# A selective-scan layer with a feed-forward layer on one core: the work behind the scan for the final 128 positions in two halves

## The reference

```python
xn = x * rsqrt(mean(x * x) + 1e-6) * norm_w
xn = xn * sigmoid((xn @ select_proj_w.T + select_proj_b) * select_gate)
xp = xn @ x_proj_w.T                       # delta | B | C, 128 columns each
delta = softplus(xp[..., :R] @ dt_proj_w.T + dt_proj_b)
A = -exp(A_log)                            # 512 x 128
def step(h, inp):                          # h: 2 x 512 x 128, one step per position
    dt, bt, ct, xt = inp
    h = exp(dt[:, :, None] * A) * h + (dt * xt)[:, :, None] * bt[:, None, :]
    return h, einsum('bdn,bn->bd', h, ct)
x1 = layernorm(x + (y + x * D_param) @ out_proj_w.T)
out = layernorm(x1 + (silu(x1 @ w_gate.T) * (x1 @ w_up.T)) @ w_down.T)   # hidden size 2048
```

## Time and profile before

| what | value |
|---|---|
| median of three runs | 2907.8 us (2907.03 to 2912.47) |
| the profiled execution, its own time | 2904.84 us |
| its span | 2902.9 us |
| mean granted TensorE clock | 0.927 of full |
| VectorE busy | 2671.0 us (92%) |
| TensorE busy | 2391.9 us (82%) |
| ScalarE busy | 1526.8 us (53%) |
| GpSimd busy | 854.6 us (29%) |
| DMA moved | 660.47 MB, mean 228 GB/s |

### The profile page before, as it was taken

How to read it: one execution, slowest core, us unless ns; L and a number is a source line. 1 busy time by engine, 2 the same in 40 slices (tenths; PEclk the granted TensorE clock), 3 DMA queues, 4 the chain that set the end, 5 groups by cost and what they waited for, 6 DMA issues and landing times.

```text
span 2902.9 us, 37666 instructions
## 1 busy us (share of the span) xinstructions
PE 2391.9 (82%) x12544; PEld 1076.6 (37%) x12544; DVE 2671.0 (92%) x4136; ACT 1526.8 (53%) x1872; POOL 854.6 (29%) x747
## 2 busy tenths in 40 slices
PE   4876678888887978889888888879788897889677
PEld 3211123444233433444234442334334442344256
DVE  2999999999998999989999999989999899999910
ACT  5553356554664456554665546655565545644432
POOL 2232232342333322332324423333223322233100
PEclk7988899999998989999899999999899998999889
DMA  3556666777666776768667676667757686677623
GB/s 128 208 208 218 215 229 209 253 241 264 228 228 229 260 265 206 253 219 290 232 210 264 234 268 228 228 236 269 263 208 251 228 283 227 229 252 251 208 74 108
DMA packets 188972, 660.47 MB, mean 228 GB/s; under 512 B 20592, under 2 KB 25712, under 8 KB 188784
## 3 DMA queue, kind: packets, MB, share of 16 engines
q1 hardware_dynamic: 152304, 544.81, 53.5%
q10 hardware_dynamic: 36480, 113.26, 11.8%
HBM read 649.60 MB, written 8.39 MB: 227 GB/s over the span
## 4 chain that ended last, share of the span: by engine, by line
PE 37%; DVE 34%; ACT 14%; issue 13%; DMA 2%; ACTq 0%; DVEq 0%
DVE h L432 22%; PE banks L656 12%; DVE banks L422 12%; PE banks L785 10%; PE banks L766 7%; PE banks L799 6%; ACT a L614 6%; ACT L442 1%; DMA w_ring<-in_gu_w 1%; DMA w_ring<-in_down_w 1%; ACT sg L580 1%; ACT L580 1%; ACT v L536 0%; ACT gated L538 0%; ACT gated L581 0%
## 5 line engine op out<-in xcount | busy, mean ns | idle before, releaser
L614 ACT ACTIVATE a<-banks 128x2048 f32<-128x2048 f32 x512 | 960.4, 1876 | 1093.9 <-PE banks L785 1024.5
L422 DVE TENSOR_TENSOR banks<-a,h 128x512 f32<-128x512 f32 x2048 | 1405.1, 737 | 55.1 <-ACT a L614 54.9
L432 DVE SCALAR_TENSOR_TENSOR h<-u_bc,BCt,banks 128x512 f32<-128x512 f32 x2048 | 1445.1, 753 | 9.1 <-PE banks L799 9.1
L377 POOL TENSOR_TENSOR dexp<-spread,dt 128x512 f32<-128x512 f32 x512 | 554.3, 1083 | 1594.9 <-DVE banks L422 1135.7
L799 PE MATMUL banks<-h,cz 128*32 128x512 f32 x4096 | 735.9, 655 | 130.6 <-DVE h L432 91.1
L785 PE MATMUL banks<-dexp,A 32*128 32x512 f32 x4096 | 634.9, 692 | 195.2 <-ACT a L614 192.5
L656 PE MATMUL banks<-vT,w_ring 128*128 128x256 f32 x2048 | 530.0, 409 | 78.7 <-ACT up L582 72.2
L656 PEld LDWEIGHTS banks<-vT,w_ring 128*128 128x128 f32 x2048 | 392.8, 200 | 299.5 <-ACT up L582 124.8
L785 PEld LDWEIGHTS banks<-dexp,A 32*128 32x128 f32 x4096 | 171.6, 196 | 527.6 <-ACT a L614 379.0
L799 PEld LDWEIGHTS banks<-h,cz 128*32 128x32 f32 x4096 | 115.0, 112 | 602.0 <-issue 531.1
L766 PE MATMUL banks<-gated,w_ring 128*128 128x256 f32 x1024 | 248.6, 389 | 11.6 <-ACT vT L588 8.9
(11 more groups left out here) (91 smaller groups left out, 1007.2 us busy)
## 6 DMA issues: line engine op xcount, KB each, us to landing
u_bc<-u_scratch SPq DMA_DIRECT2D x1024, 512.0 KB, 4.5
w_ring<-in_gu_w ACTq DMA_DIRECT2D x128, 512.0 KB, 5.0
w_ring<-in_down_w ACTq DMA_DIRECT2D x64, 512.0 KB, 5.1
U<-in_xT ACTq DMA_DIRECT2D x8, 512.0 KB, 5.3
x_tok<-in_x_rows SPq DMA_DIRECT2D x16, 256.0 KB, 4.9
out_rows<-v ACTq DMA_DIRECT2D x16, 256.0 KB, 3.9
u_scratch<-t_exp ACTq DMA_DIRECT2D x8, 256.0 KB, 5.3
u_scratch<-t_one ACTq DMA_DIRECT2D x8, 256.0 KB, 4.7
```

Source lines behind the costliest of these rows:

```text
L377: e.tensor_tensor(dexp[:, q % E_RING, :, :].rearrange("p (b t) j -> p b t j", b=BATCH), spread[:, :].unsqueeze(1).unsqueeze(1).to_broadcas ...
L422: e.tensor_tensor(m_ps[:, b, :], a[blk % 2][:, b, s, :], h[:, (t - 1) % H_RING, b * D:(b + 1) * D], ALU.mult).then_inc(s_m, 1)
L432: e.scalar_tensor_tensor(h[:, t % H_RING, part], u_bc[:, t % U_RING, part], BCt[c % 2][:, 0, b * TB + tl:b * TB + tl + 1], m_ps[:, b, :], ...
L614: e.activation(dst, src.rearrange("p g (r j) -> p g r j", j=GP), ACT.Exp, scale=-1.0).then_inc(s_exp, 1)
```

## The change

The work behind chunk 7 is split by windows. Window 14 (unit x = 7 of the new code, `LAST`) is done beside the scan, in the second half of chunk 7, from slot 132 on. Window 15 (unit x = 8) alone is left for the tail. Each has 128 columns where a unit had 256, and each loads all 24 weight tiles for itself.

Window 14 has no buffers of its own: its hidden values lie in `w_sel`, its rows in `U`, its transposed rows in `w_xp`, and its tiles in a ring of three places (part of `w_xp`, an idle `dt`, `t_both`). Window 15's tiles lie in the two buffers `a`, 16 places: eight are loaded from position 1018 on, eight more and the last eight in the tail. The unit behind chunk 6 (x = 6) starts at slot 0 of chunk 7 instead of slot 8, and its gaps are shorter (`wide` is 0): a `gu` tile moves the thread by 5 slots instead of 6, a `down` pair of tiles by 9 instead of 11. A unit of 128 columns moves it by 3 and by 5.

The first lines of `stages_behind` are written anew too. The second window's `xd` and `ya` pieces now both carry the star, and stand in an order of their own, so that `yt` of window 0 no longer comes behind them: this goes for every chunk from 1 to 6 as well.

```diff
+TILES_14 = 3
+TILES_IN_A = 8
+def halves(x):
+    return (0, 1) if x < LAST else (x - LAST,)
-def stages_behind():
-    yield from [("tile", 0, 0), ("tile", 1, 0), ("xd", 0, 0), ("ya", 0, 0), ("xd*", 1, 0), ("ya", 1, 0)]
-    for w in range(2):
-        yield from [("yt", w, 3), ("ymc", w, 2), ("outp", 2 * w, 3), ("outp", 2 * w + 1, 4), ("ln1", w, 2 * w)]
+def stages_behind(x):
+    both, ws, wide = x < LAST, halves(x), int(x < LAST - 1)
+    ahead = W_RING if both else (TILES_14 if x == LAST else HB)
+    if x <= LAST:
+        for j in range(ahead):
+            yield "tile", j, 0
+    for w in ws:
+        yield from [("xd", w, 0), ("ya", w, 0)] if w == ws[0] else [("xd*", w, 0), ("ya*", w, 0)]
+    for w in ws:
+        yield from [("yt", w, 2 + wide), ("ymc", w, 2)]
+        if x == UNITS - 1:
+            for j in range(TILES_IN_A, HB):
+                yield "tile", j, 0
+        yield from [("outp", 2 * w, 3), ("outp", 2 * w + 1, 3 + wide), ("ln1", w, 2 * w if both else 4)]
+    first, second = (2, 2 + wide) if both else (0, 2)
     for hb in range(HB):
-        yield from [("gu", 2 * hb, 2), ("gu", 2 * hb + 1, 3), ("act", hb, 1)]
+        yield from [("gu", 2 * hb, first), ("gu", 2 * hb + 1, second), ("act", hb, 1)]
...
-            yield "down", 4 * m + q, 2 + q % 2
+            yield "down", 4 * m + q, (2 + q % 2 * wide if both else 1)
...
-    if c > 0:
-        threads.append([(8 if c == LAST else 0), list(stages_behind())])
+    if c == LAST:
+        threads.append([2 * SLOTS * GP + 4, LAST, list(stages_behind(LAST))])
+    if c > 0:
+        x = c - 1 if c < CHUNKS else LAST + 1
+        threads.append([0, x, list(stages_behind(x))])
...
+            columns = 2 * P if stage in ("gm", "gp") and x >= LAST else 4 * P
+            while taken.get(group, 0) + columns > 4 * P:
                 group += 1
...
+                if t == SEQ - BS + 2:
+                    for j in range(TILES_IN_A):
+                        behind(LAST + 1, "tile", j)
```

More of the change, by code:

```diff
@@ L214, in build @@
         d_w = [sem(f"d_w{i}") for i in range(W_RING)]
+        d_w14 = [sem(f"d_w14_{i}") for i in range(TILES_14)]
+        d_w15 = [sem(f"d_w15_{i}") for i in range(2 * TILES_IN_A)]
         s_const, s_ident, s_zero, s_spread, s_gates, s_A = (
@@ L624, in scalar @@
             for slot in sorted(plans[-1]):
-                for stage, j in plans[-1][slot]:
-                    before(0, stage, j)
+                for stage, x, j in plans[-1][slot]:
+                    before(x, stage, j)
                     if stage == "x_in":
@@ L821, in tensor @@
                         y_row(t - 1)
-                    for stage, j in plans[c].get(SLOTS * (t % TB) + i, ()):
-                        behind(c - 1, stage, j)
-                        before(c + 1, stage, j)
+                    for stage, x, j in plans[c].get(SLOTS * (t % TB) + i, ()):
+                        behind(x, stage, j)
+                        before(x, stage, j)
             y_row(SEQ - 2)
@@ L828, in tensor @@
             for slot in sorted(plans[CHUNKS]):
-                for stage, j in plans[CHUNKS][slot]:
-                    behind(LAST, stage, j)
+                for stage, x, j in plans[CHUNKS][slot]:
+                    behind(x, stage, j)
         block = ctx.enter_context(nc.Block())
```

330 lines of the change are left out of this document (204 added, 126 removed).

## The result

The changed kernel takes 2891.88 us (median of seven runs, 2883.55 to 2903.78), the kernel before 2907.8. The ratio is 0.9948, 95% interval 0.9928 to 0.9968: half a per cent faster, where 2.7% were forecast. The profiled execution is one of the seven, at 2883.55, beside 2904.84 before. It is 21.3 us shorter.

The account below looks back on a forecast made before the run. VectorE bounds the scan, losing little to TensorE's work, bank waits and clock; the tail is a separate chain. 2904.84 - 63 (tail) + 22 (chunk 7) - 36 (chunks 1 to 6) = 2828, stated as 2829 us, range 2782 to 2872.

Parts of the forecast that it names:

- Tail, -63: Work after the last scan position: head, tiles and end together -66.9, +4 against it, so 63 us shorter.
- The halving: Tail tiles: 128 columns instead of 256 take half the TensorE time, 1.86 us each; -49.5 for 24 tiles.
- 15.5 - 5.5: End of the tail: 15.5 us before, less 5.5 because one `ln2` falls away.
- 16.4 + 4: Head of the tail, up to the first tile: 16.4 us for one window, plus an allowance of 4.
- The +4: Head of the tail: window 14's late work and eight loads hold up TensorE and ScalarE; +4 us (0 to 10).
- Chunk 7, +22: Last scan chunk: denser tiles and window 14 raise TensorE's demand by block, costing 22 us (0 to +55).
- the DMA bound of +11: Chunk 7, window 14's loads: if 320 GB/s were all, they take 93 us for 82, +11.
- I take half of the 12.5 as regained: 6 x 6 = -36: Chunks 1 to 6: moving the second softplus set regains half of blocks 9 and 10's 12.5 us; -36 in all.
- the stall: Chunks 1 to 6: VectorE's loss of 15.5 us each, 12.5 in blocks 9 and 10, laid to late TensorE.
- the bounds ran from 0 to -75: Limits on the chunks 1 to 6 gain: nothing regained (0) or the whole 12.5 us a chunk (-75).
- The first softplus set takes over the stall: Rival, 15%: in chunks 1 to 6 the set in block 5 costs the time instead, no gain there; 2865 us.
- The slower rival: Rival, 3%: both softplus sets cost 12.5 us in all six middle chunks, +75 for -36; 2940 us.

Follow-up runs that it names:

- e6: Changed kernel with two places for window 15's tiles instead of sixteen, so two loads ahead instead of eight; 2922.13 us in one execution, tail 103.6.
- a_again: The changed kernel profiled once more with nothing altered; 2890.39 us, chunk 7 at 362.1.
- e2: Kernel before with only the star on the second window's `ya` added; 2927.39 us, ratio 1.0067.
- e7: Changed kernel without window 14's tile loads from the fourth on, so stale weights are used; 2886.0 us in one execution, chunk 7 at 359.8.
- e8: Changed kernel with a gap ahead of the `gu` tiles in chunks 1 to 6, restoring the old places from there on; 2930.98 us in one execution.
- e5: Changed kernel with the softplus sets moved to slot 14 of blocks 5 and 9, which moved the first tile too; 2921.63 us, ratio 1.0054.
- e1: Changed kernel with the second window's `ya` star taken back in chunks 1 to 6, restoring their old order; 2870.17 us, ratio 0.9866.
- e3: Changed kernel with six ring places for `dexp` instead of four, and four for `u_bc` instead of five; 2873.61 us, ratio 0.989.
- e13: Changed kernel with four places for `u_bc` alone, `dexp` still four; 2894.14 us in one execution.
- e12: Kernel before with six places for `dexp` and four for `u_bc`, nothing of the change; 2886.72 us, ratio 0.9926.
- e10: e4 with the `gu` tiles of chunks 1 to 6 two slots later; 2914.47 us, ratio 1.0026.
- e11: e4 with the `gu` tiles of chunks 1 to 6 one slot later; 2843.81 us in one execution.
- e4: Changed kernel with the old order in chunks 1 to 6, six places for `dexp` and four for `u_bc`; 2844.89 us, ratio 0.9785.

## Why the prediction was wrong

It gave 2829 with a range of 2782 to 2872; 2891.88 is outside by 20. "Faster" was right, by 16 us where 79 were forecast.

- **Tail, -63: right** (-64.9). The halving held and the price of a tile was a little high: with the clock at full a half-width tile takes 39.27 / 22 = 1.79 us for 1.86 forecast. The first two lay mostly in a stretch at 1.2 GHz and took 6.58 together, 3.0 more than two others, where the forecast gave 2 for one slow one. The two errors cancel in the 46.1. The tiles' stretches, the busy time of each engine on them and the granted clock:

```profile
2825.45:2832.03 6.58, 6.58 (x33) 6.58 (x34) 0.00 (x0) 0.00 (x0) 0.53 0.21 68
2832.03:2871.30 39.27, 39.27 (x354) 39.27 (x352) 0.00 (x0) 0.00 (x0) 1.00 0.29 97
```

 The end has 10.0, from 2871.51 on, as forecast (15.5 - 5.5). The head, from the last sum's end at 2805.74 to the first tile at 2825.45, has 19.7 for 16.4 + 4. The +4 was near in size and wrong in its reason: nothing of window 14 stands in the chain. The transposition takes 2.06 there and the first half of the output projection 3.54, where the chain of before had 1.14 and 1.96, and the granted clock goes with it: mostly at 1.2 GHz after, at 2.4 before. The stretches, of after and then of before (the clock is the third number from the end):

```profile
2806.00:2815.00 9.00, 6.64 (x17) 3.51 (x15) 1.03 (x2) 1.69 (x3) 0.00 (x0) 0.62 0.59 214
```

```profile
2762.00:2775.00 13.00, 7.60 (x30) 4.01 (x30) 2.83 (x5) 5.82 (x12) 0.00 (x0) 0.99 0.26 82
```

 That makes 2.5 us of the 3.3. TensorE had been idle 1.47 us ahead of 2805.88 and 1.58 ahead of 2808.52, where in before it was 0.84 and 0.28 at the same two places; whether that is why the clock was down I did not test. e6 shows that the loads ahead are a condition.
- **Chunk 7, +22: near** (+15.1; +19 in a_again, up to +27 in the other kernels with this plan). By e7 the DMA bound of +11 is not there. The sum left out the star in this chunk, which alone takes 8.6 off (e2). Against e2's 334.5 the denser plan costs 23.7, close to the 22 that was summed up for it; that the star's gain is still in there is not shown, so part of the nearness may be luck.
- **Chunks 1 to 6, "I take half of the 12.5 as regained: 6 x 6 = -36": the step that failed**; it was +26.4. Its first half held: the second softplus set no longer stops block 9. From the end of block 8 of after on, ScalarE's set runs in the hole that the order showed, and the next exponentiation follows it at once:

```profile
1607.49 0.84 ACT L593 ACTIVATE pre<-banks,vec 128x256 f32<-128x256 f32 x2
...
1613.48 1.86 ACT L735 ACTIVATE a<-banks 128x2048 f32<-128x2048 f32 x1
...
1616.65 0.38 ACT L703 ACTIVATE sg<-banks 128x256 f32<-128x256 f32 x1
```

 Blocks 9 and 10 took 30.5 + 22.4 before (chunk 6) and take 21.0 + 22.7 after (chunk 4): 9.2 us less a chunk, some 55 in six, more than the 36. So the other blocks must have lost some 82, and for that the sum had no term.

 Two things of the same step did not hold. First, it took all of the loss for waits. VectorE's other loss, products stretched by GpSimd, was in the trace of before (49 of the 97 us above 2.52 a position) and was read as part of "the stall"; so I had no term for it that could grow, and the bounds ran from 0 to -75 with no loss in them. It grew to 111 us, while the waits fell from 48 to 13. Second, it took an earlier place of a stage for free apart from the softplus sets. e2 shows that the new order alone costs 29.7 on the kernel before, e8 that it costs some 10 us a chunk already with the part ahead of the tiles, of which I had priced nothing.
- **The rivals.** None was it. "The first softplus set takes over the stall" (2865) asked for waits of 12.5 a chunk behind it; block 5 has 21.0, block 6 has 24.2, and all waits of six chunks are 10.9. What of block 6's loss is the set's is not told apart; e5 gained nothing by moving it, but moved the tiles too. The slower rival had its loss in both softplus sets; the loss of after is spread over eleven blocks, most of them without a set.
- **The distance between the profiled execution and the median**, which I took as 1 to 3 us, was 8 after, some 7 of the error of 63; the middle chunks are 62 of it, the start 2, and chunk 7 and the tail take 9 off.

What is shown: that the order makes the loss (e1, e2), that `dexp` released late by TensorE makes most of the collisions (e3, e13, the rows), and that waits take their place in part when they are gone (e3, e12). What is only argued: that TensorE is late in blocks 1, 3 to 8, 10 and 11 because of the stages' new places, and how much its granted clock adds to that; I traced single cases. What stays open: which phases of a plan are good. No rule by the softplus sets' place alone or by the parity of the slot fits the runs, and one slot, e10 against e11, moves the time by 70 us. About 10 us of e1's middle chunks above before, with the same order in its programs there, are not explained either; with the ring of six only 3 are left of them (e4 against e12).

## What to carry to other kernels

Ahead of a change to an order, split the loss of the bounding engine in two, time that it waits and time that its own instructions take above their best, and count by step, so that the parts add up: here a gain in the first was paid in the second, and back again with a deeper ring. An engine that is placed beside another by a wait on it keeps its place only as long as its other waits are met early, so give its ring enough depth (two more places were worth 21 us before the change, 18 after it). Where several stages share one bank, a plan is an edge: measure its neighbours by one slot, and change a part of the program that the change needs apart from one that it does not need (the split and what goes with it in chunk 7 were worth 42 us, the star that came along in chunks 1 to 6 cost about 20).

## What the runs showed of the hardware

GpSimd's and VectorE's instructions on two operands in SBUF did not slow each other a little; they took turns. In the rows above, GpSimd's piece of 1574.10 ended at 1575.37, and the pair of products begun at 1574.47 ended at 1576.52, 1.15 us behind it, nearly the 1.29 of a pair alone: it stood until the piece was through. The other way round, the `dexp` of 1572.80, begun 0.44 us ahead of the end of a pair at 1573.24, took 1.34 instead of its 1.05, and ended 0.90 after it. Both are the rule in the trace of after: of 153 pairs begun while a piece had 0.23 us or more to go, 117 ended 1.15 to 1.18 us behind that piece, and all 36 `dexp` begun in a pair's second product, 0.15 us or more ahead of its end, ended 0.89 to 0.91 behind it. The sum, which reads one of its large operands from a bank of PSUM, kept its 1.39 beside GpSimd's pieces. The Trainium skill says this in "SBUF — State Buffer", section "SBUF: two separate sides": the port pair that GpSimd shares with VectorE is an exclusive lock, taken by a VectorE instruction with two SBUF inputs against a GpSimd instruction that reads SBUF, and the other blocks for the whole instruction. By that rule each pair could lose up to the length of a piece, 1.05 to 1.8 us; the trace agrees, with 0.76 and 1.08 lost in the two pairs shown and the two constant distances. The page bears on the very term that failed, and the prediction did not use it.

DMA moved more than in any stretch that I had seen before: while the last layer norm of the head ran, the loads of window 15's tiles kept the DMA engines busy all the time. The stretch, with the busy time of TensorE, its weight loads, VectorE, ScalarE and GpSimd, granted clock, DMA share and GB/s:

```profile
2815.00:2822.60 7.60, 2.46 (x6) 0.76 (x4) 0.00 (x0) 4.84 (x10) 0.00 (x0) 0.92 1.00 398
```

398 GB/s over 7.6 us, at a share of 1.00, is 6% above the 376 that the prediction worked out from 320 at 0.85. The Trainium skill's 358 ("DMA: Bandwidth & Descriptors", Specifications) is passed here, so it was no limit for this kernel, which runs on one core, in a stretch of this length.
